# A perceiver layer on one core: context scores and weighted sums as plain fp32 matmuls instead of split ones

## Chip, core and metric

The kernel runs on one core of a Trainium2 chip. The metric is the device time of one execution in microseconds (us), the median of the runs shown.

## The reference

Three residual sublayers, over x of 128 batches x 32 rows x 256 and a context of 128 batches x 257 rows x 192, all fp32:

```
x = x + xattn(layernorm(x), ctx)      # 8 heads of 64, softmax over the 257 context rows, bias bo
x = x + recurrence(layernorm(x))      # sigmoid decays, state (1-w)*S + k v^T over the 32 rows, 4 heads of 64
x = x + ffn(layernorm(x))             # low rank: U1 (256x64), V1 (64x1024), gelu, U2, V2

q = x @ Wq ; k = ctx @ Wk ; v = ctx @ Wv
out = softmax(q k^T / 8) v ; y = out @ Wo + bo
```

## The kernel before

The 128 batches go in 16 groups of 8 (G = 8), so a group has 256 rows of x. The three sublayers form a pipeline over groups: while group g+2 is in the cross attention (`ga`), group g+1 is in the recurrence (`gp`) and group g in the feed-forward part (`gc`). A phase is one turn of this: "a", "ab", 14 times "abc" (the loop), "bc", "c".

The cross attention never forms k and v. Wk is folded into the query: Qk = q Wk^T, 192 values per head and query, so a batch has 8 heads x 32 rows = 256 queries (two blocks r of 128) against its 257 context rows. The weighted sum of the context (`acc`, 192 x 256) is projected by Wv afterwards, per group (WV).

Every engine runs its own program written out by hand, and the engines meet in semaphores. All of them follow the same lists. START is the part of a turn before the batches: WV0, WV1, XT, XT3, Pf, q0, q1, H0, H1, Y1, Qk0 ... Qk7 among others, z. Their outputs go to four PSUM banks (`gb`) in turn; a step waits until the bank's last user has drained it. Then come `score(0)`, Qf, and eight batch steps b (L633 on): `turn_probs(b)` transposes the probabilities, `score(b + 1)` makes the next batch's scores, a piece of filling work of the recurrence follows (FILL1: projections k, r, v in steps 0 to 2, S tiles in 3 to 6, O2 in 7), then `pv(b)` makes the weighted sum.

For one batch, before the change:

- SyncE loads the context twice: transposed (`raw_t`, 192 x 257, the last 64 rows twice, on both halves of the partitions) and natural (`raw_n`, 2 x 128 rows x 192). Both have two buffers. Its queue has the order load_t(b), load_n(b), and each waits until GpSimd is done with the buffer (`tlo_ready`, `nlo_ready`).
- ACT rounds them to float32r (`t_hi` L671, `n_hi` L681), GpSimd subtracts to get the low parts (`t_lo` L1072, `n_lo` L1080).
- `score(b)` (L437) is five float32r matmuls for each of two query blocks: Qk hi and lo against context hi, Qk hi against context lo, and two against `t1`, in which hi and lo of the last 64 context columns share the 128 partitions. Behind each block stands a short matmul that transposes the previous batch's last probability column (`tailp`).
- DVE takes the row maximum (`nmaxs` L882), ACT the exp (`exps` L687), DVE scales by the reciprocal sum (`norm_probs` L888) and splits the 257th column (`tail_parts` L896).
- after the transposes into `ptp`, ACT copies out `pth` (L700), DVE the rest `ptl` (`pt_lo` L903), and `pv(b)` (L474) is ten float32r matmuls and two for the 257th row (`tailc` x `ptt`).
- ACT copies `acc` to `pc` (L704). Qk heads are likewise written in two parts, `qk_h` by ACT (L726) and `qk_l` by DVE (L979); the bank is free after the second.

GpSimd also does the products `rhat` and `khat` of the recurrence ("hats", L1102), ordered among the batch steps, `xb`, `ob` and the rstd chain; DVE does the decay steps of GAPS (`bw` L948, `k1` L953, masked copies of S tiles L995) between its batch work.

Other matmuls (q, Qk, WV, Y1, projections) are plain fp32. K=64 matmuls of two heads go in pairs to the upper and lower half of the array's rows (L432, L433), WV to halves of its columns (L503).

Of the kernel before, what the change touches and what calls it, by code (L numbers as in the profile page):

```python
# [172 lines left out]
def build(nc, a, out):  # L173
    with ExitStack() as ctx:
# [28 lines left out]
        t0h = [sb(f"t0h{i}", [P, LP], F32R) for i in range(2)]  # L203
        t0l = [sb(f"t0l{i}", [P, LP], F32R) for i in range(2)]
        t1 = [sb(f"t1_{i}", [P, LP], F32R) for i in range(2)]
        t1s = sb("t1s", [P, LP], F32R)

        nat = [sb(f"nat{i}", [P, LT, 384], F32R) for i in range(2)]
# [26 lines left out]
        def at_(name, shape, dt, offset):  # L235
# [18 lines left out]
        qk_h = at_("qk_h", [P, 2, G, 256], F32R, 16 * KB)  # L254
        qk_l = at_("qk_l", [P, 2, G, 256], F32R, 32 * KB)
# [60 lines left out]
        def _(sp):  # L316
# [3 lines left out]
            def body(ph):  # L320
# [44 lines left out]
        def _(pe):  # L365
            mm = nc.tensor.matmul

            def body(ph):
# [57 lines left out]
                def qk(p):  # L426
# [10 lines left out]
                def score(b):  # L437
                    pe.wait_ge(s["tlo_ready"], ga.at(G, b + 1))
# [4 lines left out]
                    if b > 1 or b == 1 and ph.which != "a":  # L443
                        pe.wait_ge(s["ptt_ready"], ga.at(G, b - 1))
                    for r in range(2):
                        o = scores[:, r, 0:LP]
                        r_ = slice(r * P, (r + 1) * P)
                        k = 0
                        for w, x in ((qk_h[:, 0, b, r_], t0h), (qk_l[:, 0, b, r_], t0h),
                                     (qk_h[:, 0, b, r_], t0l), (qk_h[:, 1, b, r_], t1),  # L450
                                     (qk_l[:, 1, b, r_], t1)):
                            last = mm(o, w, x[b % 2][:], start=k == 0, stop=k == 4)  # L452
                            k += 1
                        if b > 0:
                            last = turn_tail(b - 1, r)
                        last.then_inc(s["scores_ready"], 1)

                def turn_tail(b, r):

                    if r == 0:  # L460
                        pe.wait_ge(s["tailp_ready"], ga.at(G, b + 1))
                    return mm(scores[:, r, 384:512], tailp[:, r], ident_r[:], start=True, stop=True)
# [11 lines left out]
                def pv(b):  # L474
                    pe.wait_ge(s["ptl_ready"], ga.at(G, b + 1))
                    pe.wait_ge(s["nlo_ready"], ga.at(G, b + 1))
                    if b % 2 == 0:
                        pe.wait_ge(tailc_in[b // 2 % 2], ga.at(16 * G // 4, 16 * (b // 4 + 1)))
                    if not (ph.which == "a" and b == 0):
                        pe.wait_ge(s["pc_ready"], ga.at(G, b))  # L480
                    n = nat[b % 2]
# [175 lines left out]
        def _(act):  # L657
            go = nc.scalar.activation

            def body(ph):  # L660
# [100 lines left out]
                if ga:  # L761
                    t_hi(0)
# [472 lines left out]
```

## Time and profile before

| | |
|---|---|
| median of 3 runs | 1336.26 us (1333.1 to 1339.06) |
| profiled execution | 1338.63 us, its span 1336.8 us |
| mean granted TensorE clock | 0.973 of full |
| busy PE (matmul) | 1109.4 us, 83%, 7880 records |
| busy PEld (weight load) | 906.3 us, 68% |
| busy DVE | 859.9 us, 64% |
| busy ACT | 788.3 us, 59% |
| busy POOL | 578.8 us, 43% |
| DMA | 73.88 MB, mean 55 GB/s; raw_t lands 2.8 us after issue, raw_n 2.4 us |

PE is TensorE, DVE VectorE, ACT ScalarE, POOL GpSimd. The shares are means over the whole span, so they don't say which engine ends last in a stage; for that one cuts out one turn of the loop (it repeats within 0.1 us) and reads its stretches, the waits, and the instructions in order of time. Rows name engine, line of the code, output and inputs; "idle before" is the wait just ahead of an instruction with what ended it. The loop turn used below runs from WV0 at 627.57 us to the next WV0 at 706.13 us.

### The profile page before, as it was taken

Reading aid. Unit: us, or ns where it says so; the run is one execution under the profiler, and the core shown is the slowest. Engines: PE = TensorE matmul, PEld = TensorE weight load, DVE = VectorE, ACT = ScalarE, POOL = GpSimd, SP = SyncE. Lnnn points to the kernel's source line nnn. Section 1 sums busy time; section 2 is a strip of 40 time slices with the busy share of each in tenths; the row PEclk is TensorE's granted clock in tenths of the full one; section 3 lists DMA queues with packets and bytes.
Section 4 is the critical chain, followed back from the end, with each engine's and each line's share of the span. In section 5 each row is a group of like instructions: output and inputs, shape, how many; then the busy total and the mean of one; then the engine's idle time right before and its main releaser. Section 6 shows DMA issues by size and latency. Waiting matters only on the chain.

```text
span 1336.8 us, 26076 instructions
## 1 busy us (share of the span) xinstructions
PE 1109.4 (83%) x7880; PEld 906.3 (68%) x7880; DVE 859.9 (64%) x2340; ACT 788.3 (59%) x1886; POOL 578.8 (43%) x788
## 2 busy tenths in 40 slices
PE   3888888888888888888888888888888888888865
PEld 2767777685767758676676767667676776767643
DVE  3548477485856749477584857748485774848542
ACT  2656575665756556575665657566575756657521
POOL 1336245372534527254263625527362553725330
PEclk9899899999999999999999999999999999989976
DMA  6211112030221202122130211213021120302000
GB/s 231 75 47 57 50 51 71 22 99 14 63 64 43 75 22 69 44 63 58 33 91 22 63 50 55 64 35 91 22 63 50 49 69 22 102 11 63 21 8 8
DMA packets 49688, 73.88 MB, mean 55 GB/s; under 512 B 5697, under 2 KB 31425, under 8 KB 49665
## 3 DMA queue, kind: packets, MB, share of 16 engines
q1 hardware_dynamic: 42464, 65.06, 16.7%
q10 hardware_dynamic: 7200, 8.53, 1.9%
q8 instruction: 12, 0.20, 0.1%
q14 instruction: 12, 0.09, 0.0%
HBM read 68.98 MB, written 4.59 MB: 55 GB/s over the span
## 4 chain that ended last, share of the span: by engine, by line
PE 31%; issue 28%; DVE 23%; ACT 10%; POOL 6%; ACTq 1%; DVEq 1%; DMA 0%; POOLq 0%; SPq 0%
DVE probs L892 7%; PE gb L523 4%; PE gb L513 4%; PE gb L432 4%; ACT probs L690 3%; DVE xn L878 3%; PE scores L452 3%; PE gb L423 3%; PE ptp L470 2%; PE acc L491 2%; DVE ptl L905 2%; DVE tailp L900 2%; PE gb L415 2%; PE gb L579 2%; PE gb L588 1%
## 5 line engine op out<-in xcount | busy, mean ns | idle before, releaser
L1092 POOL TENSOR_TENSOR rstd<-ve,vecs 128x2 f32<-128x2 f32 x48 | 35.3, 736 | 395.8 <-DVE ve L869 395.8
L1075 POOL TENSOR_TENSOR t0l<-raw_t,t0h 128x258 fp32r<-128x258 f32 x128 | 95.2, 744 | 247.7 <-ACT t1s L679 247.7
L491 PE MATMUL acc<-pth,nat 128*128 128x256 f32 x768 | 172.8, 302 | 33.6 <-DVE ptl L905 33.2
L690 ACT ACTIVATE probs<-scores,nmax 128x257 f32<-128x257 f32 x256 | 119.1, 471 | 98.0 <-DVE nmax L885 97.8
L491 PEld LDWEIGHTS acc<-pth,nat 128*128 128x128 f32 x768 | 126.4, 188 | 48.4 <-DVE ptl L905 36.7
L470 PE MATMUL ptp<-ident_r,probs 128*128 128x128 f32 x512 | 84.3, 288 | 68.5 <-DVE probs L892 66.9
L491 PE MATMUL acc<-ptl,nat 128*128 128x256 f32 x512 | 137.4, 280 | 0.0
L979 DVE TENSOR_TENSOR qk_l<-gb,qk_h 128x512 fp32r<-128x512 f32 x128 | 83.8, 687 | 79.4 <-ACT qk_h L726 78.5
L702 ACT ACTIVATE pth<-ptp 128x512 fp32r<-128x512 f32 x128 | 76.6, 598 | 87.5 <-PE ptp L470 87.5
L706 ACT ACTIVATE pc<-acc 128x512 f32<-128x512 f32 x128 | 76.5, 598 | 81.2 <-PE acc L491 77.4
L892 DVE TENSOR_SCALAR probs<-probs,rinv 128x257 f32<-128x257 f32 x256 | 120.2, 511 | 4.5
L995 DVE COPY_PREDICATED s<-mask,gb 128x256 f32<-128x256 uint8 x256 | 113.7, 446 | 11.9 <-issue 6.3
L470 PEld LDWEIGHTS ptp<-ident_r,probs 128*128 128x128 f32 x512 | 56.8, 143 | 93.3 <-DVE probs L892 91.6
L885 DVE TENSOR_REDUCE nmax<-scores 128x1 f32<-128x257 f32 x256 | 97.4, 416 | 22.6 <-PE scores L452 21.1
L1083 POOL TENSOR_TENSOR nat<-raw_n,nat 128x256 fp32r<-128x256 f32 x128 | 95.6, 747 | 35.7 <-ACT nat L685 35.7
L905 DVE TENSOR_TENSOR ptl<-ptp,pth 128x512 fp32r<-128x512 f32 x128 | 87.6, 684 | 35.0 <-ACT pth L702 35.0
L726 ACT ACTIVATE qk_h<-gb 128x512 fp32r<-128x512 f32 x128 | 69.4, 595 | 68.0 <-PE gb L432 68.0
L985 DVE TENSOR_TENSOR x<-gb,xb 128x512 f32<-128x512 f32 x16 | 11.1, 692 | 149.7 <-PE gb L513 149.7
L491 PEld LDWEIGHTS acc<-ptl,nat 128*128 128x128 f32 x512 | 96.6, 189 | 1.2
L452 PE MATMUL scores<-t0h,qk_h 128*128 128x258 f32 x256 | 89.7, 350 | 5.8 <-DVE qk_l L979 5.8
L1077 POOL TENSOR_TENSOR t<-raw_t,t1s 128x258 fp32r<-128x258 f32 x128 | 91.3, 714 | 0.0
L432 PE MATMUL gb<-qs,wk 64*128 64x256 f32 x256 | 71.3, 400 | 19.6 <-DVE qk_l L979 16.6
(131 smaller groups left out, 3328.7 us busy)
## 6 DMA issues: line engine op xcount, KB each, us to landing
raw_t<-in_ctx_t SPq DMA_DIRECT2D x128, 258.0 KB, 2.8
raw_n<-in_ctx_n SPq DMA_DIRECT2D x128, 192.0 KB, 2.4
xin<-in_x SPq DMA_DIRECT2D x16, 256.0 KB, 2.9
out<-vt ACTq DMA_DIRECT2D x16, 256.0 KB, 3.5
tailc<-tail_scratch SPq DMA_DIRECT2D x64, 6.0 KB
wq<-in_wq SPq DMA_DIRECT2D x1, 512.0 KB, 3.7
wk_raw<-in_wk SPq DMA_DIRECT2D x1, 512.0 KB, 4.2
wo<-in_wo ACTq DMA_DIRECT2D x1, 512.0 KB, 5.2
```

What stands on the lines that cost most here:

```text
L432: last_even = mm(even[:, c], wk[0:64, p, c_], qs[0:64, p], start=True, stop=True)
L452: last = mm(o, w, x[b % 2][:], start=k == 0, stop=k == 4)
L470: last = nc.tensor.transpose(ptp[:, t, r * P:(r + 1) * P], probs[:, r, t * P:(t + 1) * P], ident)
L491: last = mm(acc[:, i], w, x, start=k == 0, stop=k == len(terms) - 1)
L690: go(probs[:, r, 0:L], scores[:, r, 0:L], ACT.Exp, bias=nmax[:, r:r + 1], accum_out=rsum[:, r:r + 1]).then_inc(s["exp_ready"], 1)
L885: v_.tensor_reduce(nmax[:, r:r + 1], scores[:, r, 0:L], AX.X, ALU.max, negate=True)\
L892: last = v_.tensor_scalar(probs[:, r, 0:L], probs[:, r, 0:L], rinv[:, r:r + 1], None, ALU.mult)
L905: v_.tensor_tensor(ptl[:], ptp[:], pth[:].bitcast(F32), ALU.subtract)\
L995: i = v_.copy_predicated(s2[:, first:first + 3:2], mask[:, l0 + l:l0 + l + 1].to_broadcast([P, 2, P]), t[:, :, l * P:(l + 1) * P])
L1075: p_.tensor_tensor(t0l[i][:], raw_t[i][:, 0], t0h[i][:].bitcast(F32), ALU.subtract)
L1077: p_.tensor_tensor(t1[i][:], raw_t[i][:, 1], t1s[:].bitcast(F32), ALU.subtract)\
L1083: p_.tensor_tensor(nat[i][:, :, 256:384], raw_n[i][:, :, 0:P], nat[i][:, :, 0:P].bitcast(F32), ALU.subtract)
```

## The change

Context, Qk and probabilities are no longer split. `score` multiplies the plain fp32 Qk (`qk`) with `raw_t` itself: for each block one matmul over 128 context columns, then, for the last 64, block 0 on partitions 0 to 63 and block 1 on 64 to 127. `pv` multiplies `raw_n` with plain `pt`: two matmuls for 128 context columns, the 257th row's matmul, then for the last 64 columns one matmul for each half of the context rows, writing to the lower and upper half of `acc`'s partitions (Wv's rows lie there twice already), and the 257th row again. The tails of the previous batch come after all score matmuls, and with b > 0 it is they that signal `scores_ready`. `t_hi`, `n_hi`, `t_lo`, `n_lo`, `pt_lo` and `qk_l` are gone; ACT's copy of a Qk head frees the bank. Loads of `raw_t` wait for the scores of the batch two before, loads of `raw_n` for its sums; TensorE waits for the loads.

```diff
 def load_t(b):
     if not (first and b < 2):
-        sp.wait_ge(s["tlo_ready"], g.at(G, b - 1))
+        sp.wait_ge(s["scores_ready"], g.at(2 * G, 2 * b - 2))
 def load_n(b):
     if not (first and b < 2):
-        sp.wait_ge(s["nlo_ready"], g.at(G, b - 1))
+        sp.wait_ge(s["acc_ready"], g.at(G, b - 1))
...
 def score(b):
-    pe.wait_ge(s["tlo_ready"], ga.at(G, b + 1))
+    pe.wait_ge(ctxt_in[b % 2], ga.at(16 * G // 2, 16 * (b // 2 + 1)))
...
+    x = raw_t[b % 2]
     for r in range(2):
-        o = scores[:, r, 0:LP]
-        r_ = slice(r * P, (r + 1) * P)
-        k = 0
-        for w, x in ((qk_h[:, 0, b, r_], t0h), (qk_l[:, 0, b, r_], t0h),
-                     (qk_h[:, 0, b, r_], t0l), (qk_h[:, 1, b, r_], t1),
-                     (qk_l[:, 1, b, r_], t1)):
-            last = mm(o, w, x[b % 2][:], start=k == 0, stop=k == 4)
-            k += 1
-        if b > 0:
-            last = turn_tail(b - 1, r)
-        last.then_inc(s["scores_ready"], 1)
+        mm(scores[:, r, 0:L], qk[:, 0, b, r * P:(r + 1) * P], x[:, 0, 0:L], start=True, stop=False)
+    for r in range(2):
+        half = slice(64 * r, 64 * r + 64)
+        last = mm(scores[:, r, 0:L], qk[half, 1, b, r * P:(r + 1) * P], x[half, 1, 0:L],
+                  start=False, stop=True)
+        if b == 0:
+            last.then_inc(s["scores_ready"], 1)
+    if b > 0:
+        turn_tail(b - 1, "scores_ready")
...
 def pv(b):
-    pe.wait_ge(s["ptl_ready"], ga.at(G, b + 1))
-    pe.wait_ge(s["nlo_ready"], ga.at(G, b + 1))
+    pe.wait_ge(s["ptev_ready"], ga.at(G, b + 1))
+    pe.wait_ge(ctxn_in[b % 2], ga.at(16 * G // 2, 16 * (b // 2 + 1)))
...
-    terms = [(0, n[:, t, lo:lo + P], p_[:, t]) for t in range(LT)
-             for lo, p_ in ((0, pth), (0, ptl), (256, pth))]
-    terms += [(1, n[:, t, P:2 * P], p_[:, t]) for t in range(LT) for p_ in (pth, ptl)]
-    terms += [(i, tailc[:, b % 4, i * P:(i + 1) * P], ptt[:]) for i in range(2)]
-    for k, (i, w, x) in enumerate(terms):
-        if k == len(terms) - 2:
-            pe.wait_ge(s["ptt_ready"], ga.at(G, b + 1))
-        last = mm(acc[:, i], w, x, start=k == 0, stop=k == len(terms) - 1)
+    n = raw_n[b % 2]
+    for t in range(LT):
+        mm(acc[:, 0], n[:, t, 0:P], pt[:, t], start=t == 0, stop=False)
+    pe.wait_ge(s["ptt_ready"], ga.at(G, b + 1))
+    mm(acc[:, 0], tailc[:, b % 4, 0:P], ptt[:], start=False, stop=True)
+    for t in range(LT):
+        mm(acc[64 * t:64 * t + 64, 1], n[:, t, P:C], pt[:, t], start=True, stop=False)
+    last = mm(acc[:, 1], tailc[:, b % 4, P:2 * P], ptt[:], start=False, stop=True)
     last.then_inc(s["acc_ready"], 1)
...
 elif n[:2] == "Qk":
     h = int(n[2])
-    go(qk_h[:, :, :, h * S:(h + 1) * S],
-       t[:].rearrange("p c (b s) -> p c b s", b=G), ACT.Copy)\
-        .then_inc(s["qkhi_ready"], 1)
+    drain(n, go(qk[:, :, :, h * S:(h + 1) * S],
+                t[:].rearrange("p c (b s) -> p c b s", b=G), ACT.Copy))
```

## Rows read from the trace of the kernel before

**Rows 1.** Stretches: START, steps 0 to 6; length, then busy (instructions) PE, PEld, DVE, ACT, POOL

```profile
627.57:659.14 31.57, 26.14 (x164) 18.09 (x163) 14.53 (x34) 19.36 (x40) 9.35 (x15) 1.00 0.08 23
659.14:665.04 5.90, 5.90 (x40) 5.54 (x41) 5.66 (x17) 4.20 (x11) 2.56 (x4) 1.00 0.02 3
665.04:670.04 5.00, 5.00 (x38) 4.79 (x36) 4.01 (x10) 4.20 (x11) 2.50 (x4) 1.00 0.30 89
670.04:676.26 6.22, 5.19 (x38) 4.78 (x37) 6.04 (x11) 4.82 (x13) 6.01 (x6) 1.00 0.40 117
676.26:682.73 6.47, 4.99 (x45) 4.38 (x45) 6.03 (x15) 3.72 (x10) 5.58 (x7) 1.00 0.26 71
682.73:688.64 5.91, 5.08 (x45) 4.42 (x45) 5.68 (x19) 3.62 (x10) 5.01 (x7) 1.00 0.30 79
688.64:693.67 5.03, 4.77 (x45) 4.37 (x45) 4.61 (x17) 3.44 (x11) 3.39 (x6) 1.00 0.49 145
693.67:700.73 7.06, 5.05 (x44) 4.38 (x45) 4.87 (x21) 2.73 (x9) 1.14 (x2) 1.00 0.33 93
...
sum 78.56, PE 67.33 PEld 55.15 DVE 53.51 ACT 49.39 POOL 36.25; mean PE 7.48 PEld 6.13 DVE 5.95 ACT 5.49 POOL 4.03
```

**Rows 2.** Waits of PE in that turn: us in total, times, longest

```profile
PE ptp L470 <- DVE probs L892: 4.2, 5, 1.2
PE acc L491 <- DVE ptl L905: 2.2, 3, 1.7
...
PE gb L432 <- DVE qk_l L979: 1.2, 2, 0.9
```

**Rows 3.** Order of time, POOL then DVE, steps 1 to 3: start, us, engine

```profile
670.25 1.64 POOL L1111 TENSOR_TENSOR rhat<-rt,fw 128x512 f32<-128x512 f32 x1 [0.66 <-ACT rt L741]
...
670.84 1.59 DVE L948 TENSOR_TENSOR at<-bwd,fw 128x512 f32<-128x512 f32 x1
...
676.58 1.20 DVE L900 TENSOR_TENSOR tailp<-probs,tailp 128x2 fp32r<-128x2 f32 x1
```

**Rows 4.** Order of time, PE, START: plain fp32 matmuls, whole, in row halves, column halves

```profile
627.57 3.67 PE L503 MATMUL gb<-pc,wv 128*64 128x256 f32 x32
...
637.95 3.72 PE L513 MATMUL gb<-wo,o 128*128 128x256 f32 x16
641.60 0.48 PE L432 MATMUL gb<-qs,wk 64*128 64x256 f32 x1
...
641.92 0.38 PE L432 MATMUL gb<-qs,wk 64*128 64x256 f32 x1
...
642.36 0.38 PE L432 MATMUL gb<-qs,wk 64*128 64x256 f32 x1
...
642.67 1.13 PE L423 MATMUL gb<-xt,wq 128*128 128x256 f32 x4
```

**Rows 5.** Order of time, PE, batch step 1: scores, projection, then sums

```profile
665.40 0.37 PE L452 MATMUL scores<-t0h,qk_h 128*128 128x258 f32 x1
...
666.85 1.94 PE L523 MATMUL gb<-xt,w 128*128 128x256 f32 x8
...
670.04 0.60 PE L470 MATMUL ptp<-ident_r,probs 128*128 128x128 f32 x4
```

**Rows 6.** Order of time, ACT then DVE, START: Qk parts, tanh, LN2 scaling

```profile
642.77 1.08 ACT L726 ACTIVATE qk_h<-gb 128x512 fp32r<-128x512 f32 x2 [2.50 <-PE gb L432]
...
654.39 0.84 ACT L733 ACTIVATE at<-gb,vecs 128x256 f32<-128x256 f32 x2 [0.87 <-PE gb L523]
...
630.58 2.11 DVE L878 TENSOR_SCALAR xn<-x,mv,rstd 128x256 f32<-128x256 f32 x2 [0.26 <-POOL rstd L1092]
...
643.40 0.69 DVE L979 TENSOR_TENSOR qk_l<-gb,qk_h 128x512 fp32r<-128x512 f32 x1 [0.99 <-ACT qk_h L726]
```

**Rows 7.** Order of time, step 6: DVE's maxima and PE's next transposes

```profile
698.35 0.74 DVE L885 TENSOR_REDUCE nmax<-scores 128x1 f32<-128x257 f32 x2
...
700.73 0.65 PE L470 MATMUL ptp<-ident_r,probs 128*128 128x128 f32 x4
```

More of the change, by code:

```diff
@@ L202, in build @@
         raw_n = [sb(f"raw_n{i}", [P, LT, C]) for i in range(2)]
[L203 to L208, printed above, removed]
         probs = sb("probs", [P, 2, LP])
         tailp = sb("tailp", [P, 2, P], F32R)
-        pth, ptl = sb("pth", [P, LT, 256], F32R), sb("ptl", [P, LT, 256], F32R)
+        pt = sb("pt", [P, LT, 256])
         ptt = sb("ptt", [P, 256], F32R)
@@ L251, in build @@
         o2 = pw[:].rearrange("p (c t) -> p c t", c=2)
-        qk_h = at_("qk_h", [P, 2, G, 256], F32R, 16 * KB)
-        qk_l = at_("qk_l", [P, 2, G, 256], F32R, 32 * KB)
+        qk = at_("qk", [P, 2, G, 256], F32, 16 * KB)
         pc = at_("pc", [P, 2, H, T], F32, 48 * KB)
@@ L444, in score, with turn_tail @@
                         pe.wait_ge(s["ptt_ready"], ga.at(G, b - 1))
+                    x = raw_t[b % 2]
                     for r in range(2):
-                        o = scores[:, r, 0:LP]
-                        r_ = slice(r * P, (r + 1) * P)
-                        k = 0
-                        for w, x in ((qk_h[:, 0, b, r_], t0h), (qk_l[:, 0, b, r_], t0h),
-                                     (qk_h[:, 0, b, r_], t0l), (qk_h[:, 1, b, r_], t1),
-                                     (qk_l[:, 1, b, r_], t1)):
-                            last = mm(o, w, x[b % 2][:], start=k == 0, stop=k == 4)
-                            k += 1
-                        if b > 0:
-                            last = turn_tail(b - 1, r)
-                        last.then_inc(s["scores_ready"], 1)
[L458 to L462, printed above, removed]
+                        mm(scores[:, r, 0:L], qk[:, 0, b, r * P:(r + 1) * P], x[:, 0, 0:L], start=True, stop=False)
[7 more added lines that the diff above has]
+                        turn_tail(b - 1, "scores_ready")
+                def turn_tail(b, done_):
+                    pe.wait_ge(s["tailp_ready"], ga.at(G, b + 1))
+                    for r in range(2):
+                        mm(scores[:, r, 384:512], tailp[:, r], ident_r[:], start=True,
+                           stop=True).then_inc(s[done_], 1)
                 def turn_probs(b):
@@ L616, in body @@
                     steps[f"q{i}"] = lambda i=i: q(i)
-                    steps[f"Qk{2 * i}"] = lambda i=i: qk(i)
+                    steps[f"Qk{2 * i}"] = lambda i=i: qk_heads(i)
                 for i in (0, 2):
@@ L638, in body @@
                         else:
-                            for r in range(2):
-                                last = turn_tail(b, r)
-                            last.then_inc(s["tailt_ready"], 1)
+                            turn_tail(b, "tailt_ready")
                     for n in FILL1[b]:
@@ L669, in drain @@
                     last.then_inc(bank_drained[bank_of(ph, name)], 1)
-                def t_hi(b):
-                    act.wait_ge(ctxt_in[b % 2], ga.at(16 * G // 2, 16 * (b // 2 + 1)))
-                    if not (ph.which == "a" and b < 2):
-                        act.wait_ge(s["scores_ready"], ga.at(2 * G, 2 * (b - 1)))
-                    go(t0h[b % 2][:], raw_t[b % 2][:, 0], ACT.Copy)
-                    if not (ph.which == "a" and b < 1):
-                        act.wait_ge(s["tlo_ready"], ga.at(G, b))
-                    go(t1s[64:128], raw_t[b % 2][64:128, 1], ACT.Copy).then_inc(s["thi_ready"], 1)
-                def n_hi(b):
-                    act.wait_ge(ctxn_in[b % 2], ga.at(16 * G // 2, 16 * (b // 2 + 1)))
-                    if not (ph.which == "a" and b < 2):
-                        act.wait_ge(s["acc_ready"], ga.at(G, b - 1))
-                    go(nat[b % 2][:, :, 0:C], raw_n[b % 2][:], ACT.Copy).then_inc(s["nhi_ready"], 1)
                 def exps(b):
@@ L698, in tail_out, with pt_out @@
                         .then_inc(s["ptt_ready"], 1)
[L700 removed]
+                def pt_out(b):
                     act.wait_ge(s["pt_ready"], ga.at(G, b + 1))
[L702 removed]
+                    go(pt[:], ptp[:], ACT.Copy).then_inc(s["ptev_ready"], 1)
                 def pc_hi(b):
@@ L765, in body @@
                         step(n)
-                    if n == "XT3" and ga:
-                        t_hi(1)
-                        n_hi(0)
                 if ga:
```

58 lines of the change are left out of this document (7 added, 51 removed).

## The prediction

> **What bounds the kernel now.** I read the stretches first. The loop over groups is periodic: one turn of its body lasts 78.56 us, of which the part that prepares scores ("START") takes 31.57 us and the eight batch steps the rest [rows 1]. TensorE is busy in nearly all of it, but not alone in setting the time. In batch steps 0 and 1 it has no gap at all (5.90 of 5.90, 5.00 of 5.00), so there any longer matmul is paid in full; steps 2, 3, 4 and 6 take 5.9 to 7.1 us with some 5.0 to 5.2 busy, so something else ends last [rows 1]. The waits of TensorE say what: in one turn it waits 4.2 us for `probs` (scaled by DVE), 2.2 us for `ptl` (DVE), and in START 1.2 us for `qk_l` (DVE) [rows 2]. DVE is thus the engine behind the gaps, and GpSimd is behind DVE: with a hat product running on GpSimd (1.64 us), DVE's `at` product takes 1.59 us, and, some steps on, the small `tailp` subtraction 1.20 us [rows 3]. That one writes two columns, so its time can't be its own work. The kernel is TensorE bound in some steps and bound by the ring scores, maximum, exp, scaling, transpose in the others.
>
> **The change, TensorE's side.** The rows name plain fp32 and split operands alike as f32, so I price by distance between starts. A plain fp32 matmul of 128x128x256 shows as two records: Y1's 8 matmuls are 16, from 637.95 to 641.60, 0.228 us each [rows 4]. A split matmul is one record: ten of them for the scores, with two short tails, go from 665.40 to 666.85, 1.45 us [rows 5]; of that I estimate 0.2 for the tails and the entry from the transposes, which stay, so the ten take 1.25, some 0.12 each. Half-array pairs (K=64, rows 0 to 63 beside 64 to 127) run side by side: two pair records are 0.44 us apart (641.92 to 642.36), so 0.22 a pair, and four take 1.07 us from 641.60 to 642.67, so going into and out of halves costs 0.19 together [rows 4]. Column halves (M=64), as in WV, take 3.67 us for 32 records, 0.115 each [rows 4].
> Scores after: 4 records x 0.228 = 0.91, two pair records 0.44, switching 0.19, tails and entry 0.2: 1.74 us against 1.45, **+0.29**.
> Weighted sums before: from 666.85 to 670.04 less 8 x 0.228 of the projection, 1.37 us [rows 5]. After: 0.91 + 0.12 + 4 x 0.115 + 0.12 = 1.61, **+0.24**.
> So TensorE gets 0.5 us more per batch where it sets the pace. No row shows plain and split matmuls mixed inside one accumulation. Bounds for that: below, the 0.19 switch of the scores is not paid (two pairs at 0.22 only), 0.3 a batch in all; above, each block pays one more switch of 0.15, 0.8 a batch. I take 0.5, nearest to the Y1, Qk and WV rows, which are the same shapes.
>
> **The other engines' side.** Gone per batch: DVE's `ptl` (0.6 to 0.7 us, as wide as `qk_l`), three ACT copies and four GpSimd subtractions; per group eight `qk_l` on DVE (0.69 each, [rows 6]). The loads now wait for scores and sums instead of GpSimd. In SyncE's queue the load of transposed context b+1 stands behind that of natural context b, which waits for the sums of b-2. It is thus issued at the start of step b-1 and needed 0.4 us into step b: one step, 5 us, for a transfer that lands in 2.8 us by the page. I cost it at nothing; without that cover it would be up to 3 us a step.
>
> **START.** Banks of Qk heads are now freed by ACT's copy (a pair takes 1.08 us from 642.77), not by DVE's `qk_l` behind it (643.40 plus 0.69) [rows 6]. I walk it: Qk0/1 end 642.67; q2 to 643.6; H2/H3 need Qk0's bank, free at 643.3, so 643.6 to 644.7; Qk2/3 to 645.7; q3 waits for H2's gelu, 645.75 to 646.7; Qk4/5 wait for Qk2's copy, which ACT does after H3's gelu, 647.1 to 648.2. The LN1 statistics no longer stand behind `qk_l`, so `xn` is ready by about 648.5, even blocked by GpSimd's `xb`. XT2, Qk6/7 follow and z starts at 650.5, its tanh at 652.55 against 654.39 [rows 6]. That is -1.85; what follows on ACT (tanh, table load, exp) is unchanged, and score(0)'s higher price hides beside it. The LN2 scaling, two operations in 2.11 us [rows 6] beside `ob` and then `t0l` on GpSimd, loses the second of these, -0.25 by estimate. START: **-2.1** (bounds 0, if ACT's order alone sets it, and -2.6).
>
> **The batch steps**, by what ends last:
> Steps 0, 1: TensorE, 5.90 and 5.00 become 6.4 and 5.5.
> Step 2 (6.22): TensorE would give 5.19 + 0.5 = 5.7, less overlaps 5.5. DVE: `at` product blocked till about 2.1, maxima 3.05, `k1` blocked by the next hat till 4.0, then the `probs` scaling meets the third hat (1.3 us long) and ends near 5.9. I take 5.95.
> Steps 3 to 5 (6.47, 5.91, 5.03): hats start after 1.25 us and are over by 3.9, before the scaling. In step 5 DVE's list has the masked copy of Sb0, which needs TensorE's filling work, ahead of the scaling; that fill moves 0.29 later, so 5.3, and TensorE's own work is 4.77 + 0.5. Steps 3 and 4 have the same content and lose their contention: 5.3 each.
> Step 6 (7.06): the copy of Sb2 stands before the maxima; +0.29 for scores, -0.6 for `ptl` gives 6.75. But the order of the sums now has the wait for `ptt` after 4 records instead of 10, with 0.7 us of work behind it instead of 0.24: 6.9.
> Step 7: part of the `ptl` waits (2.2 us in a turn, three times [rows 2]) goes, 0.24 comes, 0.
> Sum 6.4+5.5+5.95+3x5.3+6.9 = 40.65 against 41.59 of steps 0 to 6 in [rows 1]: **-0.95**. As a check of the ring in a step without interference: from the start of the maxima to the next transposes is 2.38 us (698.35 to 700.73) [rows 7], plus 0.41 transposes and 1.74 scores and 0.15 latency, 4.7, under 5.3.
>
> **A rule of the skill.** The rows show blocking, not sharing: the `at` product starts 0.6 us after a hat and ends 0.6 us after it [rows 3]. The Trainium skill (SBUF — State Buffer, Who interferes with whom) says that a DVE operation with two SBUF inputs and a GpSimd operation exclude each other for a whole instruction, and that issue order decides. The trace agrees. By it the hats that remain still block step 2; with bandwidth merely shared step 2 would be 5.5 and the turn 0.45 us shorter, 7 us in all.
>
> **Sum.** One turn -2.1 - 0.95 = -3.05. 14 such turns: -42.7; the turn with two groups in flight has no LN2, -2.75; the first, with no filling work and START half at the low clock, -1.0. Together -46.4 on the profiled execution's 1338.6 us: 1292. The profiled run lies 2.3 us above the median 1336.26, so the forecast for the median is **1290**.
>
> **The rivals.**
> A (forecast), 0.52: 1272 to 1306.
> B, the relief is worth more: START -2.6, steps 3 to 5 at 5.2, step 2 at 5.5, and the switch of 0.19 not paid in seven steps (-1.3): -5.6 a turn, about 1250. For: the waits of [rows 2] are all DVE's. Against: the hats stay. 0.15.
> C, switching costs more: 0.3 more in each of seven steps, +2.1 a turn, so -0.95 x 15: 1322. For: no row shows the mixing. 0.14.
> D, slower: the halves do not run side by side once they accumulate onto an open group. Scores then pay 0.44 more, sums 0.45, 0.9 in steps 0, 1 and 6, 0.45 in 2 and 7, 0.65 in 3 to 5: +5.5, turn +2.5, 1374. It decides from about 1.0 us more TensorE time per batch than now. Against: the Qk and WV rows, the latter accumulating. 0.12.
> E, the edit leaves no mark: relief and price cancel, or raw buffers arrive late and eat the gain: 1330 to 1342, 0.07.
>
> **How the numbers follow.** Faster by over 0.5% (about what a measurement of this kernel can tell from no change): A, B, nearly all of C: 0.80. Same: 0.07. Slower: 0.13. The range leaves out D, and the far end of E: 1248 to 1332.
>
> **What would show it.** Right: TensorE's waits for `probs` in steps 3 and 4 gone, `tailp` near 0.16 us, z's tanh 1.8 us earlier, steps 0 and 1 longer by 0.5, a turn near 75.5 us. Wrong: pair records of the new K=64 scores further apart than 0.22, column halves further than 0.12, waits for the context loads at TensorE, or a step 2 that is not shortened.

## The result and the profile after

Measured over 18 runs of each kernel: before 1334.67 us (1330.86 to 1339.06), after 1326.95 us (1319.24 to 1334.62), a ratio of 0.9941 with the interval 0.9927 to 0.9955. The change makes the kernel faster, by 0.6%: the sign of the forecast, a sixth of its size (8 us for 46). 1326.95 lies inside the range 1248 to 1332, nearest to rival C (1322). One of the ten runs of experiment 7 took 2272.89 us with the full clock granted, and is left out of its median.

The profiled execution took 1328.87 us (span 1327.1). The first part of its page, busy time, share and records of each engine:

```profile
span 1327.1 us, 23547 instructions
PE 1194.7 (90%) x7368; PEld 845.4 (64%) x7368; DVE 636.4 (48%) x2083; ACT 621.4 (47%) x1502; POOL 245.3 (18%) x276
```

All that the change takes off the other engines is gone: DVE from 859.9 to 636.4 us, ScalarE from 788.3 to 621.4, GpSimd from 578.8 to 245.3. TensorE got 85 us more. The relief is real, and TensorE's own work took nearly all of it back. The same stretches as in [rows 1], START, steps 0 to 7 (length; busy and instructions of PE, PEld, DVE, ACT, POOL; granted clock):

```profile
622.11:651.09 28.98, 25.92 (x162) 17.82 (x161) 9.29 (x26) 17.67 (x37) 5.47 (x9) 1.00 0.05 13
651.09:657.97 6.88, 6.88 (x36) 5.11 (x37) 5.61 (x16) 3.07 (x8) 0.00 (x0) 1.00 0.00 0
657.97:663.94 5.97, 5.97 (x34) 4.34 (x32) 3.20 (x10) 3.11 (x8) 0.26 (x1) 1.00 0.26 77
663.94:669.91 5.97, 5.97 (x34) 4.35 (x34) 5.00 (x11) 3.07 (x8) 3.92 (x3) 1.00 0.40 121
669.91:675.38 5.47, 5.47 (x41) 3.86 (x41) 2.84 (x11) 2.36 (x7) 2.50 (x2) 1.00 0.28 85
...
680.86:686.34 5.48, 5.48 (x41) 3.88 (x41) 3.56 (x16) 2.36 (x7) 0.00 (x0) 1.00 0.31 85
686.34:694.03 7.69, 6.00 (x42) 4.02 (x41) 4.60 (x22) 2.36 (x7) 0.00 (x0) 0.96 0.42 128
694.03:700.87 6.84, 6.84 (x42) 5.37 (x41) 1.09 (x6) 2.64 (x5) 0.70 (x1) 0.80 0.14 38
sum 78.76, PE 74.01 PEld 52.63 DVE 39.43 ACT 38.99 POOL 15.34; mean PE 8.22 PEld 5.85 DVE 4.38 ACT 4.33 POOL 1.70
```

Read the second column against the first: in steps 0 to 5 they are equal, so TensorE has no gap left and sets each of these times. Step 6 alone has one, and in the last two rows the granted clock is below 1. The waits of TensorE in that turn (in total, times, longest), to hold beside [rows 2]:

```profile
PE acc L478 <- ACT ptt L669: 1.7, 1, 1.7
PE ptp L463 <- DVE probs L854: 1.4, 1, 1.4
PE gb L569 <- ACT xt L693: 0.7, 1, 0.7
```

The wait for `probs` is down from five times to the one behind START, that for `ptl` is gone with the tile, and in its place stands one for `ptt`, the transposed tail column. The gap itself isn't new: in step 6 the kernel before waits as long, for `ptl`, ahead of its first matmul of the sums:

```profile
698.49 0.39 PE L491 MATMUL acc<-pth,nat 128*128 128x256 f32 x1 [1.71 <-DVE ptl L905]
```

In both kernels DVE's list has the masked copy of Sb2 at the head of that step, in front of `ptl` and the maxima before the change and of the maxima alone after it. Steps 6 and 7 of TensorE after the change, in order of time:

```profile
689.83 1.13 PE L476 MATMUL acc<-pt,raw_n 128*128 128x256 f32 x4
692.65 0.39 PE L478 MATMUL acc<-ptt,tailc 128*128 128x256 f32 x1 [1.69 <-ACT ptt L669]
692.97 0.75 PE L480 MATMUL acc<-pt,raw_n 128*64 128x256 f32 x4
693.65 0.58 PE L481 MATMUL acc<-ptt,tailc 128*128 128x256 f32 x1
694.03 1.06 PE L463 MATMUL ptp<-ident_r,probs 128*128 128x128 f32 x4
```

After a gap of 1.69 us the four transposes take 1.06 us instead of 0.60: the granted clock is at its lower level (1.2 of 2.4 GHz) for 3.4 us. The trace has such a stretch in 12 of the 14 loop turns, each beginning 0.2 to 1.3 us after the gap has ended. In the turn before 464.56 us it is absent, and its steps 6 and 7 read:

```profile
451.59:459.03 7.44, 5.75 (x41) 3.87 (x41) 4.51 (x21) 2.36 (x7) 0.00 (x0) 1.00 0.44 133
459.03:464.56 5.53, 5.53 (x42) 4.11 (x41) 1.17 (x6) 2.52 (x5) 0.70 (x1) 1.00 0.20 49
```

12.97 us against 14.53: the clock costs 1.56 us a turn, some 19 us of the whole. Without it a turn is 77.2 us. In the kernel before, a gap of the same length (1.71 us) is followed by a low stretch in 2 of its 14 turns only.

**The price on TensorE.** Step 3 in order of time. PE first, then its weight loads; "[0.33 <-issue]" is idle time of the load unit just before, which waited for nothing that the profile shows:

```profile
669.91 0.60 PE L463 MATMUL ptp<-ident_r,probs 128*128 128x128 f32 x4
670.34 1.03 PE L440 MATMUL scores<-raw_t,qk 128*128 128x257 f32 x4
671.30 0.70 PE L443 MATMUL scores<-raw_t,qk 64*128 64x257 f32 x4
671.94 0.44 PE L454 MATMUL scores<-ident_r,tailp 128*128 128x128 f32 x2
672.31 0.37 PE L538 MATMUL gb<-rhat,khat 64*128 64x128 f32 x1
...
673.40 1.13 PE L476 MATMUL acc<-pt,raw_n 128*128 128x256 f32 x4
674.18 0.47 PE L478 MATMUL acc<-ptt,tailc 128*128 128x256 f32 x1
674.57 0.65 PE L480 MATMUL acc<-pt,raw_n 128*64 128x256 f32 x4
675.16 0.39 PE L481 MATMUL acc<-ptt,tailc 128*128 128x256 f32 x1
675.38 0.27 PE L463 MATMUL ptp<-ident_r,probs 128*128 128x128 f32 x1
```

```profile
671.30 0.30 PEld L443 LDWEIGHTS scores<-raw_t,qk 64*128 64x128 f32 x4 [0.33 <-issue]
671.94 0.30 PEld L454 LDWEIGHTS scores<-ident_r,tailp 128*128 128x128 f32 x2 [0.33 <-issue]
674.57 0.20 PEld L480 LDWEIGHTS acc<-pt,raw_n 128*64 128x64 f32 x4 [0.23 <-issue]
675.15 0.19 PEld L481 LDWEIGHTS acc<-ptt,tailc 128*128 128x128 f32 x1 [0.39 <-issue]
```

From the first score matmul to the first S tile is 1.97 us (670.34 to 672.31), from the first matmul of the sums to the next transposes 1.98 (673.40 to 675.38). In steps 0 and 1, where TensorE set the time before and after, the two together cost 0.98 and 0.97 us more than in [rows 1] (6.88 for 5.90, 5.97 for 5.00); the forecast had 0.5. The second fence shows where it sits. Between matmuls of one geometry the next weights are loaded beside the running matmul, with no such gap (the loads of L440 and L476 here). At each change between the whole array and halves of it they are not: the load stands at the start of its matmul (674.57 and 674.57, 675.15 and 675.16) after a gap of 0.2 to 0.4 us. The Trainium skill (TensorEngine Tiling (Array Packing), Key Properties) says that a change of tiling mode drains TensorE. The trace agrees: four such gaps a batch here, 0.23 to 0.39 us each.

### The profile page after: what moved, and what is told of

It is laid out like the page before. It is cut to its first block, busy times and chain, and to the rows that moved or that the text cites. A ratio compares the mean times of both kernels' runs of the same rounds, so it can differ in the third digit from the quotient of the medians.

```text
span 1327.1 us, 23547 instructions
## 1 busy us (share of the span) xinstructions
PE 1194.7 (90%) x7368; PEld 845.4 (64%) x7368; DVE 636.4 (48%) x2083; ACT 621.4 (47%) x1502; POOL 245.3 (18%) x276
## 4 chain that ended last, share of the span: by engine, by line
PE 40%; issue 36%; POOL 8%; ACT 8%; DVE 6%; ACTq 1%; DMA 0%; POOLq 0%; SPq 0%; DVEq 0%
PE gb L513 7%; PE gb L503 4%; PE scores L440 4%; PE gb L416 4%; PE scores L443 3%; POOL khat L1051 3%; PE gb L425 3%; PE gb L578 2%; PE acc L476 2%; PE ptp L463 2%; PE acc L480 2%; POOL rstd L1024 2%; POOL rhat L1043 2%; PE gb L569 1%; PE scores L454 1%
## 5 line engine op out<-in xcount | busy, mean ns | idle before, releaser
L476 PE MATMUL acc<-pt,raw_n 128*128 128x256 f32 x512 | 140.1, 396 | 0.6 <-ACT pt L674 0.6
L440 PE MATMUL scores<-raw_t,qk 128*128 128x257 f32 x512 | 132.2, 381 | 1.4 <-ACT qk L698 1.4
L476 PEld LDWEIGHTS acc<-pt,raw_n 128*128 128x128 f32 x512 | 90.9, 190 | 20.2 <-issue 3.2
L440 PEld LDWEIGHTS scores<-raw_t,qk 128*128 128x128 f32 x512 | 88.5, 190 | 9.3 <-issue 1.7
L674 ACT ACTIVATE pt<-ptp 128x512 f32<-128x512 f32 x128 | 76.0, 594 | 37.3 <-PE ptp L463 35.9
L698 ACT ACTIVATE qk<-gb 128x512 f32<-128x512 f32 x128 | 69.8, 606 | 49.2 <-PE gb L425 49.1
L443 PE MATMUL scores<-raw_t,qk 64*128 64x257 f32 x512 | 90.2, 429 | 0.0
L480 PE MATMUL acc<-pt,raw_n 128*64 128x256 f32 x512 | 85.9, 415 | 0.0
L1043 POOL TENSOR_TENSOR rhat<-rt,pw 128x512 f32<-128x512 f32 x48 | 67.8, 1413 | 94.6 <-DVE pw L925 94.6
L538 PE MATMUL gb<-rhat,khat 64*128 64x128 f32 x512 | 76.2, 292 | 6.9 <-POOL khat L1051 6.9
L540 PE MATMUL gb<-rhat,khat 64*128 64x128 f32 x512 | 76.2, 292 | 0.0
```

The lines of the kernel that those rows point to most:

```text
L440: mm(scores[:, r, 0:L], qk[:, 0, b, r * P:(r + 1) * P], x[:, 0, 0:L], start=True, stop=False)
L443: last = mm(scores[:, r, 0:L], qk[half, 1, b, r * P:(r + 1) * P], x[half, 1, 0:L], start=False, stop=True)
L476: mm(acc[:, 0], n[:, t, 0:P], pt[:, t], start=t == 0, stop=False)
L480: mm(acc[64 * t:64 * t + 64, 1], n[:, t, P:C], pt[:, t], start=True, stop=False)
L1043: i = p_.tensor_tensor(rhat[:, l], rt_[:].rearrange("p c t -> p (c t)"), (pw if l else fw)[:], ALU.mult)
```

## Experiments

Each ran beside the kernel before on the same chip; ratios are to that. "The change" is the kernel after.

**1. The copy of Sb2 moved.** In step 6 of the change, ScalarE's `ptt` comes late. DVE's list has the masked copy of Sb2 ahead of the maxima.

```diff
-[["Sb2"], ["Sb3"], [], []],
+[[], ["Sb2", "Sb3"], [], []],
```

> The changed kernel, with DVE's masked copy of Sb2 moved from ahead of the maxima of step 6 to behind them. Theory 1 (the wait costs twice: in step 6 TensorE waits 1.69 us for ptt, and from there the granted clock is at its lower level for a stretch in 12 of 14 turns, which makes a turn 78.76 us instead of 77.21): the wait goes, the low stretches of the loop go too, a turn is about 75.5 us, the kernel about 1285 us, ratio to before 0.963. Theory 2 (the low stretches have nothing to do with this wait): only the wait goes, a turn is shorter by 1.5 to 1.7 us, about 1303 us, ratio 0.976, with low stretches still once a turn. Theory 3 (TensorE's work alone fills the turn): under 5 us gained.

1299.38 us (1295.76 to 1300.87), ratio 0.9709 [0.9674, 0.9744]. In step 6 the 1.69 us for `ptt` are replaced by this on the next transposes:

```profile
602.13 0.66 PE L463 MATMUL ptp<-ident_r,probs 128*128 128x128 f32 x4 [0.59 <-DVE probs L854]
```

The turn is 76.08 us (two WV starts, 531.65 and 607.73), and the trace has no low-clock stretch within the loop. That is the first theory's mechanism, at a time nearer to the second's. One edit in DVE's order is worth 27.6 us. Within the loop the two profiled executions differ by 34.5 us: 16 from the shorter turn (77.21 to 76.08, 14 times) and 19 from the twelve stretches. Outside the loop the execution of this run is 6 us longer, with more of it at the low clock.

**2. The same edit on the kernel before**, to see what of experiment 1 belongs to the change.

> The kernel before, with only Sb2's masked copy moved behind the maxima of step 6. It says what that order is worth without the change. Step 6 was 7.06 us with 5.05 of TensorE work, its waits 1.7 us for ptl and 0.2 for ptt. If the order is the cause there too, step 6 falls to 5.2 to 5.5 us, 1.6 x 15 = 24 us, ratio 0.982; the clock was at its high level in nearly all turns, so nothing more is to be had from it. If the step was bound by DVE's whole work, under 8 us.

1315.81 us (1313.62 to 1316.82), 0.9865 [0.9848, 0.9883]; the turn 77.31 us. It helps there too, by 1.35%, though less. Step 6 falls from 7.06 to 5.80 us: the copy was the cause of the wait for `ptl` there, as it is of the one for `ptt` after the change. With the edit in both kernels the change is worth 0.9709/0.9865 = 0.984, so 1.6% and not 0.6%: step 6 and the clock behind it had been hiding one per cent.

**3. The 257th row's matmuls at the end of the sums**, so that the first of them starts 0.86 us later in a step without a wait.

```diff
-    mm(acc[:, 0], tailc[:, b % 4, 0:P], ptt[:], start=False, stop=True)
     for t in range(LT):
-        mm(acc[64 * t:64 * t + 64, 1], n[:, t, P:C], pt[:, t], start=True, stop=False)
+        mm(acc[64 * t:64 * t + 64, 1], n[:, t, P:C], pt[:, t], start=False, stop=False)
+    mm(acc[:, 0], tailc[:, b % 4, 0:P], ptt[:], start=False, stop=False)
```

> The changed kernel, with the two matmuls of the 257th row at the end of the weighted sums, behind the column halves (one accumulation group for the whole bank). If each change between split (float32r) and plain fp32 matmuls costs TensorE time, the sums fall from 1.98 us to about 1.7 us a step. If only the change between whole array and column halves costs, they fall by under 0.15 us. The wait for ptt in step 6 becomes some 1.1 us instead of 1.69 in either case. If the low clock behind step 6 depends on how long TensorE waits there, the low stretches in the loop go: 1327 minus 9 for the wait, minus 0 to 30 for the mixing, minus another 18 for the clock, so about 1298 with the clock and without the mixing.

1304.18 us (1300.71 to 1306.8), 0.9782 [0.9756, 0.9808]. Steps 1 and 3 to 5 stay at 5.97 and 5.48 us, so the order inside the sums costs TensorE nothing. The wait remains, shorter:

```profile
523.82 0.39 PE L480 MATMUL acc<-ptt,tailc 128*128 128x256 f32 x1 [1.11 <-ACT ptt L669]
```

The turn is 76.77 us, 0.44 under the change's undisturbed one, and there is no low-clock stretch within the loop. 0.44 x 14 is 6 us of the 22.8 gained; the other 17 are about what twelve stretches at 1.56 us cost (19). That is the cleanest measurement of the clock's part.

**4. The row halves last among the scores**, so that the S tiles, themselves row halves, follow without a change of geometry.

```diff
+    if b > 0:
+        turn_tail(b - 1, None)
     for r in range(2):
         half = slice(64 * r, 64 * r + 64)
         last = mm(scores[:, r, 0:L], qk[half, 1, b, r * P:(r + 1) * P], x[half, 1, 0:L],
...
-    if b > 0:
-        turn_tail(b - 1, "scores_ready")
```

> The changed kernel, with the previous batch's tails between the whole-array score matmuls and the row halves, so that in steps 3 to 6 the row halves of the scores run straight into the row halves of the S tiles. If each change between whole array and row halves costs 0.1 to 0.15 us, steps 3 to 5 fall from 5.48 us to about 5.2 us while steps 0 to 2 stay: 1.0 to 1.2 us a turn, 15 us in all; about 1311, ratio to before 0.98. If the price of the tails (0.37 us for two short matmuls) is their own and not one of switching, steps 3 to 5 stay at 5.4 to 5.5 us and the time at 1325.

1304.42 us (1303.32 to 1308.45), 0.9775 [0.9757, 0.9792]. Steps 3 to 5 take 5.21 us for 5.48. Two changes of geometry are gone there: out of the row halves to the tails, and back into them for the S tiles. The 0.27 us are not all that the two cost, for `ptt` now comes later: ahead of the 257th row's first weights the load unit waits 0.26 us for it, and the sums take 2.11 us for 1.98. Experiment 5 has that wait away. Steps 1 and 2, where whole-array projections follow, have as many changes as in the change itself and go from 5.97 only to 5.92. This run still has low-clock stretches in seven of its 14 turns, with the gap for `ptt` at 1.69 us in all.

**5. All three edits.**

> The changed kernel with three orders mended: Sb2's masked copy behind the maxima of step 6, the sums' tails last, the scores' row halves last. From 1299.4 us for the first alone: minus 12 to 18 for the row halves, minus 3 to 30 for the sums. If TensorE alone sets the steps, 1275 to 1285; if the ring of scores, maximum, exp and scaling takes over (4.7 us by the old rows, with steps 3 to 5 near 5.1), still 1280; under 1270 only if mixing split and plain matmuls was dear.

1265.57 us (1264.22 to 1271.25), 0.948 [0.9463, 0.9497]: 5.2% faster than before. Steps 3 to 5 take 5.08 us, step 6 5.84, the turn 74.33 us. Only the last theory allowed for less than 1270, and by a dear mixing of split and plain matmuls, which experiment 3 excludes. What makes up the rest: with the sums' tails last, nothing waits for `ptt` in steps 3 to 5, and the two changes of geometry saved there are worth 5.48 less 5.08, 0.40 us, so 0.20 each.

**6. A second pass over each Qk head on DVE**, which frees the bank, as before the change.

```diff
+dve.wait_ge(s["qkhi_ready"], ga.at(H, h + 1))
+drain(n, v_.tensor_tensor(qk_l[:, :, :, h_], t[:].rearrange("p c (b s) -> p c b s", b=G),
+                          qk[:, :, :, h_], ALU.subtract))
```

> The changed kernel, with DVE's second pass over each Qk head put back (it subtracts into a tile that nobody reads, and frees the bank). If the 2.6 us by which the part before the batch steps became shorter come from the freed bank chain, that part goes back to about 31.3 us from 28.98 and the kernel is 2.3 x 15 = 35 us slower than the changed one, about 1360 us, ratio to before 1.02. If they come from the idle GpSimd and the shorter scaling, it stays within 0.5 us and the kernel is within 8 us of the changed one.

1361.59 us (1361.09 to 1362.04), 1.0183 [1.0151, 1.0216]. START as in the first row above:

```profile
638.49:669.61 31.12, 26.43 (x161) 17.80 (x160) 13.43 (x34) 18.11 (x37) 5.47 (x9) 1.00 0.03 12
```

31.12 us for 28.98, and 31.57 in [rows 1]. So 2.1 of START's 2.6 us come from DVE's pass over the Qk heads being gone, as forecast. The run puts back both what the pass does, its work on DVE and its hold on the bank, so it doesn't say how much is the bank's alone.

**7. GpSimd's four subtractions per batch brought back**, on data that nobody uses, with nobody waiting for them.

> The changed kernel with GpSimd's four subtractions a batch put back on idle data (same shapes, in the same places of its list; nobody waits for them, results unused). If my term was right that steps 2 to 5 got shorter through less blocking of DVE by GpSimd, they get longer again by 0.3 to 1 us, 1340 or more. If TensorE's own work fills the steps now, DVE's scalings go back from 0.35 to about 0.5 us each and no step of 0 to 5 moves by more than 0.1: within 5 us of the changed kernel, step 2 included.

1333.83 us (nine runs, 1330.59 to 1337.88), 0.9997 [0.9978, 1.0015]. The change's whole gain is gone. DVE's group rows (busy, mean ns of one), first of this run, then of the change:

```profile
L856 DVE TENSOR_SCALAR probs<-probs,rinv 128x257 f32<-128x257 f32 x256 | 106.6, 459 | 4.8 <-DVE rinv L854 0.3
L864 DVE TENSOR_TENSOR tailp<-probs,tailp 128x2 fp32r<-128x2 f32 x128 | 42.7, 334 | 4.4
```

```profile
L854 DVE TENSOR_SCALAR probs<-probs,rinv 128x257 f32<-128x257 f32 x256 | 79.1, 352 | 4.5
L862 DVE TENSOR_TENSOR tailp<-probs,tailp 128x2 fp32r<-128x2 f32 x128 | 20.9, 164 | 4.4
```

Steps 3 and 4 grow to 6.01 and 5.99 us, with waits for `probs` of 0.39 and 0.31 us; steps 1 and 2 stay at 5.97, so the first theory holds for two of its four steps. The turn is 78.36 us where the undisturbed one of the change is 77.21: 1.15 us. Two of its 14 loop turns have a low-clock stretch where the change has twelve, though the wait for `ptt` is still 1.69 us in each; that gave back what the longer turn lost, and the loop of the profiled execution takes 1099.7 us for 1099.6. Why the same gap is followed by the low clock in one kernel and mostly not in the other stays open.

**8. The change without its column halves.** It leaves the last 64 columns of the context out of the weighted sums.

```diff
-for t in range(LT):
-    mm(acc[64 * t:64 * t + 64, 1], n[:, t, P:C], pt[:, t], start=True, stop=False)
-last = mm(acc[:, 1], tailc[:, b % 4, P:2 * P], ptt[:], start=False, stop=True)
+last = mm(acc[:, 1], tailc[:, b % 4, P:2 * P], ptt[:], start=True, stop=True)
```

> The changed kernel without the two matmuls on column halves in the weighted sums (the last 64 context columns are left out of them, but for the 257th row), which prices them with all that hangs on them. My sum had 0.46 us a step (4 records at 0.115). If entering and leaving the halves costs as it does for row halves, steps 0 to 5 fall by about 0.7 us, from 5.97 to 5.3 and from 5.48 to 4.8 or where the ring takes over (4.9). At 0.46 they fall to 5.5 and 5.0.

1279.34 us (1276.46 to 1281.09), 0.9581 [0.9544, 0.9619]. Steps 1 and 3 of a turn:

```profile
633.22:638.41 5.19, 5.19 (x29) 4.16 (x28) 2.90 (x10) 2.74 (x8) 0.00 (x0) 1.00 0.31 89
644.02:649.47 5.45, 4.91 (x36) 3.69 (x37) 3.41 (x14) 2.75 (x8) 2.49 (x2) 1.00 0.32 86
```

The first, bound by TensorE as it was, lost 0.78 us for four records that I had priced at 0.46. The second lost 0.02: the ring with DVE's `probs` holds it (0.54 us of wait), so that the same saving is worth nothing there.

**9. The change without its row halves.** It leaves the last 64 columns out of the scores.

```diff
-for r in range(2):
-    half = slice(64 * r, 64 * r + 64)
-    last = mm(scores[:, r, 0:L], qk[half, 1, b, r * P:(r + 1) * P], x[half, 1, 0:L],
-              start=False, stop=True)
```

> The changed kernel without the two row-half matmuls of each batch's scores: it leaves the last 64 columns of the context out of the scores, so its result isn't the reference's. If the halves cost what the forecast gave them (0.115 each, 0.23 a batch), steps bound by TensorE fall by 0.23 and the turn by some 1.6 us: 1300. If entering and leaving them is the price (0.63 for the pair with the switch, and 0.1 to 0.2 more for the tails behind them), steps 1 and 2 fall by 0.5 to 0.8 us, as they did without the column halves, and the time is near 1280.

1251.06 us (1248.38 to 1254.28), 0.9362 [0.9318, 0.9406]. Steps 1 and 3, with step 7 below:

```profile
620.02:625.16 5.14, 5.14 (x29) 4.13 (x28) 3.20 (x10) 3.10 (x8) 0.26 (x1) 1.00 0.30 90
...
630.30:634.95 4.65, 4.65 (x38) 3.66 (x38) 3.23 (x13) 2.36 (x7) 2.50 (x2) 1.00 0.39 100
...
650.93:658.03 7.10, 7.10 (x42) 5.45 (x41) 1.16 (x6) 2.64 (x5) 0.70 (x1) 0.76 0.15 41
```

0.83 and 0.82 us less (the change has 5.97 and 5.47), where the forecast had 0.44 for the matmuls and 0.19 for the switching (the first theory above gives its price too low). The time fell below what either theory had put down: the saving of 0.8 us was paid out in all steps that TensorE bounds, since the ring with `probs`, which held experiment 8 at 5.46, has lost the same 0.8 us here, the row halves being part of it. This holds although 8 of the 14 turns have two low-clock stretches and two have one (0.76 in the last row).

**10. The scores half of the change alone**, with sums and probabilities as before.

> The kernel before with the scores' half of the change alone: plain Qk and transposed context, row halves, Qk banks freed by ACT; the sums stay split (n_hi, n_lo, ptl). If the parts add up, it gets all of START's gain (2.6 us a turn) and pays 0.42 us in the steps that TensorE fills. If DVE's ptl still sets the steps 2 to 6, those stay near their old lengths plus 0.4: about -1 us a turn, 1320. If what is left of DVE's work now fits under TensorE's, steps 3 to 5 go to 5.2 and the time to about 1300.

1303.19 us (1302.3 to 1303.93), 0.9759 [0.9726, 0.9793]: more than the whole change gives. TensorE waits 42.9 us for `probs` and 29.2 for `ptl` in it. The undisturbed turn is 76.49 us, 0.72 under that of the change, and step 6 has its gap here too (1.71 us, for `ptl`), followed by a low stretch in 4 of 14 turns only. Of the 24 us between the two kernels the shorter turn thus makes 10, the clock most of the rest.

**11. The sums half alone.**

> The kernel before with the sums' half of the change alone: plain natural context and probabilities, column halves; scores, Qk and transposed context stay split. START keeps its 31.6 us. Steps 0 and 1 pay 0.46 us each, steps 2 to 5 lose ptl (0.7 us of DVE) and pay 0.46. If the low clock comes with the wait for ptt behind four records in step 6, its stretches appear in the loop here too, one a turn, and not in the scores' half: about 1335 to 1345 with them, 1320 without.

1495.47 us (1489.98 to 1499.15), 1.1191 [1.1139, 1.1244]: a large miss. One row of the waits (in total, times, longest) names a transfer:

```profile
ACT t0h L672 <- DMA raw_t<-in_ctx_t: 191.2, 79, 4.3
```

The load of `raw_t` for b + 1 stands in SyncE's queue behind that of `raw_n` for b, which now waits for sums; with split scores ScalarE wants `raw_t` two steps ahead.

**12. The sums half with the loads in another order.**

```diff
+load_t(2)
 for b in range(2, G):
-    load_t(b)
+    if b + 1 < G:
+        load_t(b + 1)
     load_n(b)
```

> Sums half of the change alone, as in the run that gave 1495 us, with one edit: SyncE issues the transposed load of the next batch ahead of the untransposed load of this one. If the 1495 us come from the transposed load queued behind the untransposed one, ScalarE's wait for raw_t (191 us in that run) falls under 40 us and the time lands between 1300 and 1350. If they come from the price of the column halves on TensorE, the time stays above 1450, with the steps no shorter.

1329.65 us (1325.32 to 1336.75), 0.9945 [0.992, 0.997]. No wait for `raw_t` is left, and 166 us went with it, so the load order was the cause, as the first theory had it, and not TensorE's price. The guess of experiment 11 that low stretches come with the sums half and not with the scores half isn't borne out: behind step 6 they stand in 4 of 14 turns here, as in experiment 10. In the whole change the same order is harmless, since there only TensorE needs `raw_t`, one step later.

**13. The scores half with the edits of experiments 1 and 4.**

> Scores half of the change alone (sums as before, with their split probabilities), with the copy of Sb2 moved from step 6 to step 5 and the row halves put last among a batch's score matmuls. If the two mends are worth here what they were worth in the whole change (27 us and 22 us of 1327), this gives 1303 less some 30 to 40: 1265 to 1275, and the sums half would be worth nothing or less. If the sums half is worth something of its own, because its short tail of VectorE takes the wait for ptl away, this stays above the whole change with all three mends (1265.6): 1275 to 1290, with waits of TensorE for ptl still there in steps 2 to 6.

1262.01 us (1259.35 to 1266.93), 0.9447 [0.9398, 0.9495]. Two starts of WV, one turn of 74.10 us:

```profile
587.92 3.67 PE L498 MATMUL gb<-pc,wv 128*64 128x256 f32 x32
...
662.02 3.67 PE L498 MATMUL gb<-pc,wv 128*64 128x256 f32 x32
```

Its interval overlaps that of experiment 5 (0.9463 to 0.9497), so the two can't be told apart. The sums half takes `ptl` off DVE and the rounding of `raw_n` off ScalarE and raises TensorE's price; in a schedule put in order the two cancel. Unlike in experiment 5, TensorE still has gaps in these steps: the transposes of steps 3 to 5 wait 0.49 to 0.61 us for `probs`.

## Why the prediction was wrong in size

The forecast turn was 75.51 us (78.56 less 3.05), the measured one 78.76. Part by part, measured less forecast:

| part | forecast | measured | off by |
|---|---|---|---|
| START | 29.47 | 28.98 | -0.49 |
| steps 0, 1 | 6.4, 5.5 | 6.88, 5.97 | +0.95 |
| step 2 | 5.95 | 5.97 | +0.02 |
| steps 3 to 5 | 3 x 5.3 | 5.47, 5.48, 5.48 | +0.53 |
| steps 6, 7, clock aside | 6.9, 5.40 | 7.44, 5.53 | +0.67 |
| low clock | 0 | 1.56 | +1.56 |
| sum | 75.51 | 78.76 | +3.24 |

**TensorE's price: the step that failed.** The mechanism was right, the terms too small: 0.98 us a batch for 0.53. Two terms are mis-sized. I took WV's 32 column-half records from [rows 4], 3.67 us, as 0.115 each; but that mean spreads the cost of one switch over 32 records, and the change has four records to a switch. Experiment 8 prices the four at 0.78 us instead of 0.46. The row halves were to cost 0.63; experiment 9 says 0.83. There I had 0.19 for going in and out, the 1.07 us from the first Qk pair to the first record behind the pairs in [rows 4], less four pairs at 0.22. That span holds only half of the price. In the traces each change of geometry lengthens two distances between starts by some 0.1 us, the one across it and the next (0.32 for 0.22 between the first two Qk pairs). The one into the pairs lies ahead of 641.60 and the last one behind 642.67: that row of four whole-array records takes 1.13 us, as L476 does in step 3 above, and L440, which follows whole-array transposes, 1.03. In and out cost 0.4, not 0.19, and experiment 5 agrees (0.40 for two changes). 0.32 and 0.20 make 0.52, which covers the 0.45 that were missing.

Both signs of being wrong that the prediction had named for these terms are there. The two pairs of the scores start 0.32 us apart (0.70 us for the row, less 0.38 for its last record), not 0.22, which is the distance within a longer run; the column halves' two pairs 0.27, so 0.13 a record and not 0.12. The bound "0.8 a batch" was crossed as well: I widened only for mixing plain and split matmuls, and experiment 3 found no cost in their order; the geometry was what changed.

**The low clock: not foreseen at all.** I did see that the sums would wait for `ptt` in step 6 and put 0.15 us on it (6.75 to 6.9), after taking 0.6 us off for `ptl`. The gap stayed as it was, 1.69 us for 1.71, since the copy of Sb2 held the maxima as it had held `ptl`, and I never asked what an idle TensorE does to its clock just ahead of a step that it bounds. In [rows 1] the granted clock is 1.00 in every step, and I read that as a property of the kernel. Nor does a turn repeat within 0.1 us throughout, as I wrote: nine of the 14 take 78.55 to 78.60 us, the other five 79.73 to 80.29, with a low stretch in each (and the turn ahead of the loop has two). In the loop that is 7.4 us of low clock before the change and 18.7 after it. Over the runs of the kernel after, times go with the mean granted clock: a span of 1317.4 us at 0.976, 1321.9 at 0.974, 1329.7 at 0.969, 1332.8 at 0.965. It also hid the change's own gain from the measurement: experiments 1 and 3 win 28 and 23 us by edits that save 1.1 and 0.4 us of a turn. What is shown is that the stretches go with the gap where it is shortened. That the gap's length alone brings them is not: gaps of 1.69 to 1.71 us in step 6 are followed by one in 12 of 14 turns of the change, in 2 of the kernel before and of experiment 7, in 4 of experiment 10 and in 7 of experiment 4.

**START: right, and a bit better.** -2.6 us for -2.1. Experiment 6 puts 2.14 on DVE's pass over the Qk heads. The tanh of z was to come 1.85 us earlier:

```profile
646.35 0.84 ACT L704 ACTIVATE at<-gb,vecs 128x256 f32<-128x256 f32 x2 [1.11 <-PE gb L513]
```

That is 24.24 us after WV's start; in [rows 6] it is 26.82 (654.39 less 627.57), so 2.58 earlier.

**The relief of DVE: right in kind, small in worth.** The waits for `probs` in steps 3 and 4 are gone and `tailp` takes 0.164 us, both as written down. Experiment 7 takes the relief back and finds 1.15 us a turn. The Trainium skill (SBUF — State Buffer, Who interferes with whom) has DVE operations with two SBUF inputs and GpSimd's exclude each other. The trace agrees: with GpSimd's idle subtractions `tailp` goes from 164 to 334 ns. Where this was to matter most, in step 2, DVE was done 0.77 us before the next transposes start (668.52 + 0.62 = 669.14, transposes at 669.91):

```profile
668.52 0.62 DVE L854 TENSOR_SCALAR probs<-probs,rinv 128x257 f32<-128x257 f32 x2
```

So TensorE set the 5.97 us, and I had the right number there from the wrong engine.

**Steps 3 to 5.** 5.3 was to come from DVE's copy of Sb0 and from TensorE's 4.77 + 0.5; TensorE's real price gives 5.48. Experiment 8 shows that the ring stands right behind, at 5.46, where my check had it at 4.7. I took the stretch from the maxima to the transposes (2.38 us) from [rows 7]. In step 3 of experiment 8 it is 3.00 us (646.47 to 649.47), because DVE's two masked copies, ahead of the scaling, wait 0.54 us for the S tiles.

**Loads.** Nothing waits for them on TensorE, as forecast. Experiment 11 shows how thin that was: the same queue order costs 166 us as soon as another engine wants the data one step sooner.

**The rivals.** C had the right cause, switching that costs more, 0.3 us in seven steps, and came within 5 us. That close it came by luck: its steps are right within 0.1 us a turn, but it had nothing for the low clock (11 us more in the loop than before) nor for START's further 0.5 us a turn (7 us less). D (halves that don't run side by side) is out by the 0.64 us of four records. B had put the relief higher; experiment 5 reaches 1265.57, but by edits outside the change.

**Does it add up?** The forecast for the profiled execution (1292) was missed by 37 us. Over the 14 loop turns the table gives 3.24 in twelve and 1.68 in the two without low clock, 42. The forecast left the kernel before its low stretches in the loop, and the kernel after has lost those 7.4 us, so 35 remain. Outside the loop the kernel gained 1.9 us where 3.75 were forecast. Together 37.

**What stays open.** What, besides a gap of 1.7 us, decides in which turns the clock falls. No run varies that alone.

## What to carry to other kernels

Price a half-array matmul with its way in and out, from a place in the trace with as few of them in a row as the change will have, measured from the last record ahead of them to the second behind them, and put those of one kind side by side: a mean over a long run hides the switch. When a change removes what the bounding engine waits for, look for what else holds the same step, for the gap can stay under another name; and look at the granted clock behind it in every turn, not in one. Measure each half of a change alone: here one half carried all of the gain, and one DVE operation in another place was worth more than the whole change.

## What the runs showed of the hardware

- A change between whole and half array costs some 0.2 us on TensorE: 0.20 by experiment 5 (5.48 less 5.08, two changes saved), 0.20 by experiment 9 (0.83 less two pairs at 0.22, halved), 0.17 by experiment 8 (0.78 less four records at 0.11, halved). The weight loads idle 0.23 to 0.39 us at those into and out of the scores' and the sums' halves.
- Four column-half records with both switches cost 0.78 us, four row-half records (two pairs) 0.83 us; inside a long run a column-half record is about 0.11.
- In 12 of 14 turns of the change a gap of 1.69 us of TensorE was followed by 3.4 us at half the clock, which cost 1.56 us each time; in the kernel before, a gap of 1.71 us at that place was in 2 of 14. With a gap of 1.11 us there (experiment 3), or of 0.59 us one place later (experiment 1), none of 14 turns had one.
- Two float32r matmuls of the 257th row stand between or behind plain fp32 ones at the same total (steps of 5.97 and 5.48 us in either order).
